# Where the expert-row buffer of a four-layer graph network is cleared: from the third layer's expert stage to the start of the program

## The chip, the cores and the metric

The kernel runs on one core of a Trainium2 chip. The metric is the device time of one execution in microseconds (us). Three runs of the kernel before gave 14256.97, 14292.15 and 14311.86 us, with a median of 14292.15 us.

## The reference, cut to what matters

Four layers follow each other over 3125 nodes with 256 float32 features and 100000 edges. Each layer is a graph part and a mixing part on the normalised nodes, and then an expert or token part. The change touches the third layer's expert part and the place where the edge lists are prepared.

```python
# third layer, expert part: E = 8 experts, hidden width 1024, the best two of 8 for each node
logits = xt @ Wr + br
probs = jax.nn.softmax(logits, axis=-1)
top_p, top_idx = jax.lax.top_k(probs, TOP_K)
weights = top_p / top_p.sum(axis=-1, keepdims=True)
...
xn = (xt - mu) * jax.lax.rsqrt(var + LN_EPS)
xe = xn[None, :, :] * ln_g[:, None, :] + ln_b[:, None, :]
h = jax.nn.gelu(jnp.einsum('end,edh->enh', xe, W1) + b1[:, None, :], approximate=False)
y = jnp.einsum('enh,ehd->end', h, W2) + b2[:, None, :]
sel = jnp.take_along_axis(y.transpose(1, 0, 2), top_idx[:, :, None], axis=1)
out = (weights[:, :, None] * sel).sum(axis=1)
```

The edges (`src`, `dst`, and two attributes `edge_attr_2` for each) are the same in all layers, so the kernel sorts them by target once, at the start.

## The kernel before, in words

`program` (L2413) holds the nodes in SBUF as X, 25 tiles of 125 nodes. It makes constants, loads x (`on_vector` "x_in", L886 with the load at L903), sorts the main edge list and the attention edge list (`sort_edges`, L107, tiles named em_ and eg_), lays out the sorted edges (`edge_rows`) and then runs eight stages in turn: the graph part and the expert part of each layer. The tiles of the stages have the prefixes a, b, c, d, e, f, g, h; the third layer's expert stage is f.

Each step of a stage is a `Block`: a piece of program for each engine, with semaphores between them. A block ends for all engines together: no engine begins the next block before every engine has got through its instructions of this one. That holds for the engine SP (SyncE) too, which does nothing but issue DMAs. It need not wait until a DMA has landed, but it must have issued it.

`sort_edges` begins with such a block. VectorE fills three tiles (L197 to L200); then SP issues the loads of `dst`, `src` and the attributes. Each array is spread over 128 partitions, 784 edges in each, which makes 127 full rows (L146, L150) and a shorter last row that is a DMA of its own (L148, L152). After these SP issues the fill of the list of edge slots in DRAM out of the tile em_pad (L154, 125 rows of 16000 bytes). VectorE waits for all six loads and then works out each edge's key (L206 on). All DMAs of SP go into one hardware queue, q1.

The third layer's expert stage, `layer2_experts` (L2193), sorts node rows by expert. Its buffers in DRAM are `f_sorted_in` and `f_sorted_out`, each 8192 + 256 = 8448 rows of 1024 bytes: 32 tiles of 256 rows, and 256 spare rows. A tile holds rows of one expert only, so some of its rows belong to no node and are cleared beforehand. The order of the stage is:

- the first block: VectorE clears the last 32 partitions of A (L2204); SP issues a DMA from one zero row in DRAM over all 8448 rows of `sorted_in` (L2208) and one over the last 256 rows of `sorted_out` (L2209), both counted on the semaphore `cleared`;
- `tile_norm` (`row_norm`, L1007 to L1018), `turn_rows` (L1047, L1056), `project` with the router's weights (loads L1088, matmuls L1098), softmax and the best two, `route` (L1936), which gives each node its two row numbers;
- the loads of the second weights w2 (L2232 to L2235), `tile_norm` on A, then `routed_rows` (L2021): GpSimd waits for `cleared` (L2033) and scatters the nodes' rows into `sorted_in` (L2036);
- `routed_experts` (L2040): 32 tiles of 256 rows through the two matrices; `joined_rows` (L2168) gathers the results.

`Scope` frees tiles and semaphores when a step ends; after 72 freed semaphores it clears them with one more barrier (L42).

Of the kernel before, what the change touches and what calls it, by code (L numbers as in the profile page):

```python
# [5 lines left out]
F32 = mybir.dt.float32  # L6
# [9 lines left out]
D = 256  # L16
# [1096 lines left out]
def put_rows(to, add=None):  # L1113

    def put(dve, t, bank, bias):
        at = to[0:NP, t, 0:bank.shape[-1]]
        if bias is not None:
            if add is None:
                return dve.tensor_tensor(at, bank, bias, ALU.add)
            dve.tensor_tensor(at, add[0:NP, t, :], bias, ALU.add)  # L1120
            dve.drain()
            return dve.tensor_tensor(at, bank, at, ALU.add)
        if add is not None:
            return dve.tensor_tensor(at, bank, add[0:NP, t, :], ALU.add)
        return dve.tensor_copy(at, bank)
    return put
# [387 lines left out]
def choose_two(nc, s, keep, lower, E, name):  # L1514
    with Scope(nc, name) as k:
        gt, eq, rank = k.sb("gt", [128, T, E, E]), k.sb("eq", [128, T, E, E]), k.sb("rank", [128, T, E])
        on_vector(nc, name, lambda dve: top_two(dve, s, gt, eq, rank, keep, lower, E))
# [75 lines left out]
def halves(xt):  # L1593
    return [xt[:, 0, :], xt[:, 1, :]]
# [338 lines left out]
F_ROOM = F_ROWS * F_TILES  # L1933
# [79 lines left out]
def expert_of(eng, tile_expert, i):  # L2013
    return eng.value_load(tile_expert[0:1, i:i + 1], min_val=0, max_val=7)


def load_first(sp, w1, w1_rows, e, i, loaded):
    sp.dma_start(w1[:, i % 2, :, :], w1_rows[bass.ds(e, 1), :, :].rearrange("a (q p) n -> p (a q) n", p=128)).then_inc(loaded[i % 2], 16)


def routed_rows(nc, A, slot, sorted_in, cleared, tile_expert, w1, w1_rows, loaded1):  # L2021

    with Scope(nc, "f_send") as k:
        scattered = k.own_sem("scattered")
        with nc.Block() as block:
            @block.sync
            def _(sp):
                for i in range(2):
                    load_first(sp, w1, w1_rows, expert_of(sp, tile_expert, i), i, loaded1)

            @block.gpsimd
            def _(pool):
                pool.wait_ge(cleared, 32)  # L2033
                for t in range(T):
                    for c in range(2):
                        pool.indirect_dma_start(sorted_in, bass.IndirectOffsetOnAxis(ap=slot[:, t, c:c + 1], axis=0), A[:, t, :], None).then_inc(scattered, 16)  # L2036
                pool.wait_ge(scattered, 16 * 2 * T)
# [152 lines left out]
                    dve.scalar_tensor_tensor(out=X[0:NP, t, :], in0=back[0:NP, n % RING, :], scalar=share[0:NP, t, c:c + 1], in1=X[0:NP, t, :], op0=ALU.mult, op1=ALU.add).then_inc(joined, 1)  # L2190


def layer2_experts(nc, I, X, const, lower):  # L2193
    with Scope(nc, "f") as k:
        gates, keep, A = k.sb("gates", [128, T, 8]), k.sb("keep", [128, T, 8]), k.sb("A", [128, T, D])
        w1, back = k.sb("w1", [128, 2, 2, 1024]), k.sb("back", [128, 8, D])
        sorted_in = nc.dram_tensor("f_sorted_in", (F_ROOM + 256, D), F32, kind="Internal").ap()
        sorted_out = nc.dram_tensor("f_sorted_out", (F_ROOM + 256, D), F32, kind="Internal").ap()
        cleared, loaded1, loaded2 = k.own_sem("cleared"), [k.own_sem(f"loaded1_{n}") for n in range(2)], k.own_sem("loaded2")
        slot, share, tile_expert = k.sb("slot", [128, T, 2], I32), k.sb("share", [128, T, 2]), k.sb("tile_expert", [1, F_TILES], I32)  # L2200
        with nc.Block() as block:
            @block.vector
            def _(dve):
                dve.memset(A[96:128, :, :], 0.0)  # L2204

            @block.sync
            def _(sp):
                sp.dma_start(sorted_in, I["zeros256"].to_broadcast([F_ROOM + 256, D])).then_inc(cleared, 16)  # L2208
                sp.dma_start(sorted_out[F_ROOM:F_ROOM + 256, :], I["zeros256"].to_broadcast([256, D])).then_inc(cleared, 16)  # L2209
        with Scope(nc, "f2") as j:  # L2210
            XT = j.sb("XT", [128, 2, N])
            tile_norm(nc, X, A, "f_norm")
            turn_rows(nc, A, XT, const, "f_turn")
            project(nc, halves(XT), I["L2_ffn_Wr"], 8, put_rows(gates), "f_g", bias=I["L2_ffn_br"])
            with Scope(nc, "f3") as s:
                total = s.sb("total", [128, T])
                softmax_of(nc, gates, 8, "f_s")
                choose_two(nc, gates, keep, lower[8], 8, "f_two")

                def shares(dve):  # L2220
                    dve.tensor_tensor(gates[0:NP, :, :], gates[0:NP, :, :], keep[0:NP, :, :], ALU.mult)
                    dve.drain()
                    normalise(dve, gates, total, 8)
                on_vector(nc, "f_sh", shares)
                route(nc, keep, gates, slot, share, tile_expert, const)
        with Scope(nc, "f4") as j:
            w2, b1, ln = j.sb("w2", [128, 8, 8, D]), j.sb("b1", [128, 8, 8]), j.sb("ln", [128, 2, 8, 2])
            with nc.Block() as block:
                @block.sync
                def _(sp):  # L2230
                    for e in range(8):
                        sp.dma_start(w2[:, e, :, :], I["L2_ffn_W2"][e, :, :].rearrange("(m p) n -> p m n", p=128)).then_inc(loaded2, 16)  # L2232
                    sp.dma_start(b1[:, :, :], I["L2_ffn_b1"].rearrange("e p m -> p e m")).then_inc(loaded2, 16)
                    sp.dma_start(ln[:, 0, :, :], I["L2_ffn_ln_g"].rearrange("e p m -> p e m")).then_inc(loaded2, 16)
                    sp.dma_start(ln[:, 1, :, :], I["L2_ffn_ln_b"].rearrange("e p m -> p e m")).then_inc(loaded2, 16)  # L2235
            tile_norm(nc, A, A, "f_norm2")
            routed_rows(nc, A, slot, sorted_in, cleared, tile_expert, w1, I["L2_ffn_W1"], loaded1)
            routed_experts(nc, sorted_in, sorted_out, w1, w2, b1, I["L2_ffn_W1"], I["L2_ffn_b2"], ln, tile_expert, A, loaded1, loaded2, const)
            joined_rows(nc, X, slot, share, sorted_out, back)
# [169 lines left out]
E_MAIN, J_MAIN, G_MAIN = 100000, 784, 125  # L2409
# [3 lines left out]
def program(nc, I, out):  # L2413
    with Scope(nc, "net") as k:
        const = dict(eye=k.sb("eye", [128, 128]), ones=k.sb("ones", [128, 128]), before=k.sb("before", [128, 128]),
                     ramp=k.sb("ramp", [128, 256]), up=k.sb("up", [128, 1]), zeros=k.sb("zeros", [1, 512]))
        lower = {4: k.sb("lower4", [128, 4, 4]), 8: k.sb("lower8", [128, 8, 8])}
        X, inv_deg = k.sb("X", [128, T, D]), k.sb("inv_deg", [128, T])
        main, gat = edge_list(nc, k, "main", G_MAIN, J_MAIN), edge_list(nc, k, "gat", G_GAT, J_GAT)
        constants(nc, const)  # L2420
        cut = k.sem("lower_cut")
        with nc.Block() as block:
            @block.gpsimd
            def _(pool):

                for n, E in enumerate((4, 8)):
                    pool.memset(lower[E][:, :, :], 1.0).then_inc(cut, 1)
                    pool.wait_ge(cut, n + 1)
                    pool.affine_select(out=lower[E][:, :, :], in_=lower[E][:, :, :], compare_op=ALU.is_gt, fill=0.0, base=0, pattern=[[1, E], [-1, E]], channel_multiplier=0)
        on_vector(nc, "x_in", lambda dve: None, loads=[(X[0:NP, :, :], table_rows(I["x"]))])  # L2430
        sort_edges(nc, main, I["src"], I["dst"], I["edge_attr_2"], E_MAIN, const, "em", inv_deg)
        sort_edges(nc, gat, I["gat_src"], I["gat_dst"], None, E_GAT, const, "eg")
        edge_rows(nc, k, main, const, "mr")
        stages = [lambda: layer0_graph(nc, I, X, inv_deg, main, const), lambda: layer0_experts(nc, I, X, gat, const, lower),
                  lambda: layer1_graph(nc, I, X, inv_deg, main, const), lambda: layer1_experts(nc, I, X, const, lower),
                  lambda: layer2_graph(nc, I, X, main, const), lambda: layer2_experts(nc, I, X, const, lower),
                  lambda: layer3_graph(nc, I, X, main, const), lambda: layer3_tokens(nc, I, X, const)]
        for stage in stages:
            stage()
        on_vector(nc, "x_out", lambda dve: None, stores=[(table_rows(out), X[0:NP, :, :])])  # L2440
# [53 lines left out]
```

## Time and profile before

| | |
|---|---|
| Runs of the kernel before | 14256.97, 14292.15, 14311.86 us |
| Execution that was profiled | 14272.68 us |
| Its span, first to last instruction | 14270.9 us |
| TensorE matmul busy | 7573.7 us (53%) |
| VectorE busy | 6386.1 us (45%) |
| GpSimd busy | 6037.2 us (42%) |
| ScalarE busy | 1225.8 us (9%) |
| Moved by DMA | 872.31 MB, 61 GB/s over the span |

All times of the trace are counted from the first instruction of the profiled execution. No engine is busy most of the time, because the stages follow each other and each is held by another engine. So a change is worth what it does to the length of the blocks it touches. A timeline row says when an instruction, or a run of equal ones, began, how long it took, and in brackets how long its engine had been idle and what ended the idle time; "<-PEq" and a line there is the end of a block. Rows marked SPq are SP issuing a DMA: their duration is the time that SP needed to issue it, not that of the transfer. In a table of windows the DMA share is the mean busy share of the 16 DMA engines.

### The profile page before, as it was taken

What the parts mean: (1) busy time and instruction counts of PE and PEld (TensorE: products, weight loads), DVE (VectorE), ACT (ScalarE), POOL (GpSimd) and SP (SyncE); (2) the same over time, 40 slices, a digit from 0 to 9 for tenths busy, and PEclk for the clock granted to TensorE, in tenths of its full rate; (3) what the DMA queues carried; (4) which work ended last, traced back from release to release, by engine and by line L of the source; (5) the groups of instructions that cost most, each with busy time, mean ns of one, the idle gap of its engine ahead of it and who ended that gap; (6) DMA issues with size and microseconds to landing.
All of it is one profiled execution on the core that took longest, in us unless ns stands there. A gap on an engine that the chain in (4) does not pass through costs nothing. (4 is left out here: it accounts for less than half of the span.)

```text
span 14270.9 us, 106989 instructions
## 1 busy us (share of the span) xinstructions
PE 7573.7 (53%) x30362; PEld 6003.4 (42%) x30362; DVE 6386.1 (45%) x16883; ACT 1225.8 (9%) x3131; POOL 6037.2 (42%) x6226
## 2 busy tenths in 40 slices
PE   3334432556665455685555564555571955666534
PEld 3333332345554355553343432433351844555423
DVE  6555654467885322320000434666632134444454
ACT  0000000000001100110000111000010210110001
POOL 1666465056662266306666003666501016666000
PEclk9999999767777555697777787777785977777767
DMA  1111111055664011103336001112503313336100
GB/s 40 55 50 56 36 55 40 19 166 170 173 176 84 10 8 8 11 23 93 92 92 85 10 6 31 45 45 46 39 9 81 111 62 95 94 94 89 26 8 15
DMA packets 455094, 872.31 MB, mean 61 GB/s; under 512 B 171930, under 2 KB 267396, under 8 KB 454154
## 3 DMA queue, kind: packets, MB, share of 16 engines
q0 software_dynamic: 277568, 621.62, 20.3%
q1 hardware_dynamic: 176960, 244.01, 5.6%
q8 instruction: 250, 4.10, 0.1%
q14 instruction: 316, 2.58, 0.1%
HBM read 821.23 MB, written 52.88 MB: 61 GB/s over the span
## 5 line engine op out<-in xcount | busy, mean ns | idle before, releaser
L552 POOL DMA_INDIRECT ee_rows<-e_table,net_mr_data x1000 | 993.5, 993 | 1271.9 <-POOLq L1405 691.3
L817 POOL DMA_INDIRECT ce_rows<-c_table,net_mr_data x1000 | 948.2, 948 | 979.8 <-SPq L810 505.8
L552 POOL DMA_INDIRECT ge_rows<-g_table,net_mr_data x1000 | 961.0, 961 | 670.8 <-issue 233.1
L387 POOL DMA_INDIRECT main_slots<-em_load,em_where x784 | 808.9, 1032 | 641.9 <-DVE em_where L362 388.5
L552 POOL DMA_INDIRECT ae_rows<-a_table,net_mr_data x752 | 726.2, 966 | 590.7 <-POOLq L1405 200.7
L552 POOL DMA_INDIRECT be_rows<-b_table,b_br_data x728 | 703.1, 966 | 428.7 <-issue 176.8
L589 PE MATMUL ee_part_ps<-ee_message,net_eye 125*125 125x256 f32 x2000 | 588.8, 459 | 451.2 <-issue 258.3
L589 PE MATMUL ge_part_ps<-ge_rows,net_eye 125*125 125x256 f32 x2000 | 626.8, 482 | 308.2 <-issue 163.3
L346 PE MATMUL em_look_ps<-em_table,em_hot_tT 25*128 25x125 f32 x1568 | 366.9, 421 | 732.1 <-issue 662.6
L828 PE MATMUL ce_part_ps<-ce_rows,net_eye 125*125 125x256 f32 x2000 | 599.2, 452 | 289.9 <-issue 195.7
L589 PEld LDWEIGHTS ee_part_ps<-ee_message,net_eye 125*125 125x125 f32 x2000 | 461.1, 235 | 560.2 <-issue 467.6
L387 POOL DMA_INDIRECT gat_slots<-eg_load,eg_where x512 | 530.3, 1036 | 387.6 <-DVE eg_where L362 226.8
L870 DVE TENSOR_TENSOR c_acc<-c_acc,ce_total_ps 125x512 f32 x125 | 86.0, 688 | 1342.2 <-remote 770.6
L589 PEld LDWEIGHTS ge_part_ps<-ge_rows,net_eye 125*125 125x125 f32 x2000 | 486.0, 250 | 418.3 <-issue 315.0
L346 PEld LDWEIGHTS em_look_ps<-em_table,em_hot_tT 25*128 25x128 f32 x1568 | 341.4, 325 | 756.9 <-issue 728.3
L828 PEld LDWEIGHTS ce_part_ps<-ce_rows,net_eye 125*125 125x125 f32 x2000 | 464.2, 233 | 400.4 <-issue 209.4
L346 PE MATMUL eg_look_ps<-eg_table,eg_hot_tT 25*128 25x125 f32 x1024 | 239.6, 421 | 472.5 <-issue 407.7
L589 PE MATMUL ae_part_ps<-ae_rows,net_eye 125*125 125x256 f32 x1504 | 423.0, 444 | 71.6 <-issue 41.8
L589 PE MATMUL be_part_ps<-be_rows,net_eye 125*125 125x16 f32 x1456 | 314.9, 365 | 262.7 <-issue 155.1
L614 PE MATMUL ae_total_ps<-ae_part,ae_hot 125*125 125x264 f32 x500 | 210.4, 561 | 441.8 <-issue 243.9
L724 DVE TENSOR_TENSOR ee_message<-ee_rows,ee_weight 125x512 f32<-125x512 f32 x500 | 309.6, 681 | 280.8 <-DMA em_key_row<-main_keys 276.6
L589 PEld LDWEIGHTS be_part_ps<-be_rows,net_eye 125*125 125x125 f32 x1456 | 314.4, 330 | 273.7 <-issue 272.1
(1010 smaller groups left out, 16655.6 us busy)
## 6 DMA issues: line engine op xcount, KB each, us to landing
em_key_row<-main_keys SPq DMA_DIRECT2D x98, 512.0 KB
f_w<-in_L_ffn_W_dram SPq DMA_DIRECT2D x40, 1024.0 KB
eg_key_row<-gat_keys SPq DMA_DIRECT2D x64, 512.0 KB
ce_rows<-c_table,net_mr_data POOLq DMA_INDIRECT x1000
ee_rows<-e_table,net_mr_data POOLq DMA_INDIRECT x1000
ge_rows<-g_table,net_mr_data POOLq DMA_INDIRECT x1000
main_slots<-em_load,em_where POOLq DMA_INDIRECT x784
ae_rows<-a_table,net_mr_data POOLq DMA_INDIRECT x752
```

The lines of the kernel that those rows point to most:

```text
L346: ins = pe.matmul(look_ps[i % 2][:, u, 0:NP], hot_tT[:, i % 2, u * 128:(u + 1) * 128], table[:, i % 2, u, 0:NP], start=True, stop=True)
L387: pool.indirect_dma_start(edge["slots"], bass.IndirectOffsetOnAxis(ap=where[:, c:c + 1], axis=0), load[:, c, :], None).then_inc(scattered, 16)
L552: pool.indirect_dma_start(rows[n][:, s, :], None, table, bass.IndirectOffsetOnAxis(ap=data[:, g, s, 0:1].bitcast(I32), axis=0)).then_inc(g ...
L589: pe.matmul(part_ps[0:NP, 0:VW], const["eye"][0:NP, 0:NP], values(g)[:, s, :], start=(s == 0), stop=(s == SLOTS - 1)).then_inc(slot_summed, 1)
L614: ins = pe.matmul(total_ps[0:NP, q, 0:WA], hot[0:NP, g % HOTS, q * NP:(q + 1) * NP], part[0:NP, g % PARTS, :], start=True, stop=True)
L724: ins = dve.tensor_tensor(message[0:NP, n, :, h * dv:(h + 1) * dv], r[0:NP, :, 0:dv], w[:, :, h:h + 1].to_broadcast([NP, SLOTS, dv]), ALU. ...
L817: pool.indirect_dma_start(rows[:, g % RING, s, :], None, table, bass.IndirectOffsetOnAxis(ap=data[:, g, s, 0:1].bitcast(I32), axis=0)).the ...
L828: pe.matmul(part_ps[g % 2][0:NP, 0:width], const["eye"][0:NP, 0:NP], rows[0:NP, g % RING, s, :], start=(s == 0), stop=(s == SLOTS - 1)).th ...
L870: dve.tensor_tensor(at, at, total_ps[g % 2][0:NP, :, 0:width], ALU.add).then_inc(added, 1)
```

## The change

The buffers and the semaphore `cleared` move from `layer2_experts` to `program`. After x has been loaded, a new block has VectorE fill a tile `blank` of 128 partitions x 22 x 256 float32 (22528 bytes in each partition) with zero. SP waits for that and issues four DMAs out of it: three over 2816 rows of `sorted_in` each, in which each partition writes 22 rows that lie behind each other, and one over the last 256 rows of `sorted_out`. Then `sort_edges` of the main list runs while `blank` still exists, and behind it a new block has SP wait for all four DMAs before the tile is given back. In the third layer's expert stage the two DMAs are gone; VectorE's clearing of A stays there. GpSimd's wait before the scatter is for 64 in place of 32.

```diff
@@ -2030,7 +2030,7 @@
-                pool.wait_ge(cleared, 32)
+                pool.wait_ge(cleared, 64)
@@ -2190,23 +2190,17 @@
-def layer2_experts(nc, I, X, const, lower):
+def layer2_experts(nc, I, X, const, lower, sorted_in, sorted_out, cleared):
...
-        sorted_in = nc.dram_tensor("f_sorted_in", (F_ROOM + 256, D), F32, kind="Internal").ap()
-        sorted_out = nc.dram_tensor("f_sorted_out", (F_ROOM + 256, D), F32, kind="Internal").ap()
...
             @block.vector
             def _(dve):
                 dve.memset(A[96:128, :, :], 0.0)
 
-            @block.sync
-            def _(sp):
-                sp.dma_start(sorted_in, I["zeros256"].to_broadcast([F_ROOM + 256, D])).then_inc(cleared, 16)
-                sp.dma_start(sorted_out[F_ROOM:F_ROOM + 256, :], I["zeros256"].to_broadcast([256, D])).then_inc(cleared, 16)
@@ -2428,12 +2422,33 @@
         on_vector(nc, "x_in", lambda dve: None, loads=[(X[0:NP, :, :], table_rows(I["x"]))])
-        sort_edges(nc, main, I["src"], I["dst"], I["edge_attr_2"], E_MAIN, const, "em", inv_deg)
+        sorted_in = nc.dram_tensor("f_sorted_in", (F_ROOM + 256, D), F32, kind="Internal").ap()
+        sorted_out = nc.dram_tensor("f_sorted_out", (F_ROOM + 256, D), F32, kind="Internal").ap()
+        cleared = k.own_sem("cleared")
+        with Scope(nc, "blank") as j:
+            share = (F_ROOM + 256) // 128 // 3
+            blank, made = j.sb("blank", [128, share, D]), j.sem("made")
+            with nc.Block() as block:
+                @block.vector
+                def _(dve):
+                    dve.memset(blank[:, :, :], 0.0).then_inc(made, 1)
+
+                @block.sync
+                def _(sp):
+                    sp.wait_ge(made, 1)
+                    for n in range(3):
+                        sp.dma_start(sorted_in[n * share * 128:(n + 1) * share * 128, :].rearrange("(p a) w -> p a w", p=128), blank[:, :, :]).then_inc(cleared, 16)
+                    sp.dma_start(sorted_out[F_ROOM:F_ROOM + 256, :].rearrange("(p a) w -> p a w", p=128), blank[:, 0:2, :]).then_inc(cleared, 16)
+            sort_edges(nc, main, I["src"], I["dst"], I["edge_attr_2"], E_MAIN, const, "em", inv_deg)
+            with nc.Block() as block:
+                @block.sync
+                def _(sp):
+                    sp.wait_ge(cleared, 64)
         sort_edges(nc, gat, I["gat_src"], I["gat_dst"], None, E_GAT, const, "eg")
```

## Rows read from the trace of the kernel before

**Rows 1.** Windows by stage: us, busy of each engine, clock, DMA share, GB/s
```profile
core 0: us, PE busy (x) PEld busy (x) DVE busy (x) ACT busy (x) POOL busy (x), PEclk, DMA share, GB/s
...
10716.00:10819.00 103.00, 0.00 (x0) 0.00 (x0) 5.42 (x2) 0.07 (x1) 0.00 (x0) 0.50 0.47 67
10819.00:11021.00 202.00, 30.46 (x154) 29.61 (x154) 65.09 (x279) 20.30 (x37) 48.32 (x51) 0.52 0.37 95
11021.00:11530.00 509.00, 466.22 (x2176) 400.86 (x2176) 59.06 (x128) 122.65 (x257) 0.04 (x1) 0.99 0.31 104
```

**Rows 2.** Timeline at the border from stage e to stage f
```profile
10708.26 6.83 DVE L1473 TENSOR_TENSOR net_X<-net_X,e_B 125x6400 f32<-125x6400 f32 x1 [0.32 <-PEq L1179]
10715.45 0.59 SPq L2208 DMA_DIRECT2D f_sorted_in<-in_zeros_dram  x1
10716.09 102.19 SPq L2209 DMA_DIRECT2D f_sorted_out<-in_zeros_dram  x1
10716.85 5.39 DVE L2204 MEMSET f_A<- 32x6400 f32 x1 [1.77 <-issue]
10818.93 1.28 ACT L999 ACT_TABLE_LOAD   x1 [124.52 <-PEq L2201]
10818.97 8.27 DVE L1007 BATCH_NORM_STATS2 f_norm_stats<-net_X 125x6 f32<-125x256 f32 x25 [96.72 <-PEq L2201]
```

**Rows 3.** Instructions on f_sorted_in: the clear and its time to landing
```profile
L2208 SPq DMA_DIRECT2D f_sorted_in<-in_zeros_dram x1: 592/592/592, 10715.5 to 10715.5; - x1
...
DMA to landing us min/median/max: 130.0/130.0/130.0
```

**Rows 4.** Timeline later in stage f: the router's loads and matmuls, GpSimd's first scatter
```profile
10845.17 0.38 SPq L1088 DMA_DIRECT2D f_g_w<-in_L_ffn_Wr_dram  x1
10845.60 0.36 SPq L1088 DMA_DIRECT2D f_g_b<-in_L_ffn_br_dram  x1
10848.63 21.17 PE L1098 MATMUL f_g_bank<-f_g_w,f_XT 128*125 128x8 f32 x100 [4.22 <-DMA f_g_b<-in_L_ffn_br_dram]
...
10951.69 1.00 POOL L2036 DMA_INDIRECT f_sorted_in<-f_A,f_slot  x1 [61.04 <-PEq L2025]
```

**Rows 5.** Timeline at the border from stage c to stage d
```profile
8329.15 6.83 DVE L1029 TENSOR_TENSOR net_X<-net_X,c_B 125x6400 f32<-125x6400 f32 x1
8337.42 8.27 DVE L1007 BATCH_NORM_STATS2 d_norm_stats<-net_X 125x6 f32<-125x256 f32 x25 [1.45 <-PEq L42]
```

**Rows 6.** Timeline at the start: the end of x's load, the edge loads, the first keys
```profile
36.45 0.71 DVE L197 MEMSET em_dst_i<- 128x784 int32 x1 [33.05 <-PEq L899]
...
39.68 0.24 SPq L146 DMA_DIRECT2D em_dst_i<-in_dst_dram  x1
...
40.43 2.67 DVE L202 MEMSET em_load<- 128x3136 f32 x1 [0.80 <-issue]
...
103.56 0.57 DVE L206 CAST em_key<-em_dst_i 128x784 f32<-128x784 int32 x1 [59.35 <-DMA em_at<-in_edge_attr_dram]
...
118.15 1.76 PE L179 MATMUL em_turn_ps<-net_eye,em_key 128*128 128x128 f32 x7 [118.15 <-DVE em_work L223]
```

**Rows 7.** Windows of single transfers: DMA share and GB/s are the last two columns
```profile
41.40:83.40 42.00, 0.00 (x0) 0.00 (x0) 2.69 (x3) 0.00 (x0) 2.76 (x2) 1.00 0.06 26
86.00:100.00 14.00, 0.00 (x0) 0.00 (x0) 0.00 (x0) 0.00 (x0) 0.00 (x0) 1.00 0.31 129
10720.00:10845.00 125.00, 7.62 (x50) 7.37 (x50) 21.33 (x74) 11.20 (x21) 0.00 (x0) 0.52 0.54 68
10908.00:10924.00 16.00, 0.00 (x0) 0.00 (x0) 0.00 (x0) 0.00 (x0) 0.00 (x0) 0.50 1.07 345
2820.00:2860.00 40.00, 0.00 (x0) 0.00 (x0) 0.00 (x0) 0.00 (x0) 0.00 (x0) 0.50 0.33 127
```

**Rows 8.** Windows of the sort of the main list and of the pause behind it
```profile
277.00:1500.00 1223.00, 463.25 (x2356) 415.43 (x2356) 641.43 (x3627) 98.20 (x98) 808.94 (x784) 1.00 0.18 52
1475.00:1521.00 46.00, 0.00 (x0) 0.00 (x0) 14.16 (x23) 0.00 (x0) 21.05 (x20) 1.00 0.11 38
```

More of the change, by code:

```diff
@@ L2196, in layer2_experts @@
         w1, back = k.sb("w1", [128, 2, 2, 1024]), k.sb("back", [128, 8, D])
-        sorted_in = nc.dram_tensor("f_sorted_in", (F_ROOM + 256, D), F32, kind="Internal").ap()
-        sorted_out = nc.dram_tensor("f_sorted_out", (F_ROOM + 256, D), F32, kind="Internal").ap()
-        cleared, loaded1, loaded2 = k.own_sem("cleared"), [k.own_sem(f"loaded1_{n}") for n in range(2)], k.own_sem("loaded2")
+        loaded1, loaded2 = [k.own_sem(f"loaded1_{n}") for n in range(2)], k.own_sem("loaded2")
         slot, share, tile_expert = k.sb("slot", [128, T, 2], I32), k.sb("share", [128, T, 2]), k.sb("tile_expert", [1, F_TILES], I32)
@@ L2435, in program @@
                   lambda: layer1_graph(nc, I, X, inv_deg, main, const), lambda: layer1_experts(nc, I, X, const, lower),
-                  lambda: layer2_graph(nc, I, X, main, const), lambda: layer2_experts(nc, I, X, const, lower),
+                  lambda: layer2_graph(nc, I, X, main, const), lambda: layer2_experts(nc, I, X, const, lower, sorted_in, sorted_out, cleared),
                   lambda: layer3_graph(nc, I, X, main, const), lambda: layer3_tokens(nc, I, X, const)]
```

## The prediction

> **What bounds the kernel now.** The chain that ended last covers only the closing 200 us, so I read the program stage by stage. First I took the windows by stage [rows 1]. The reader is to see a hole: from 10716 to 10819 us TensorE, ScalarE and GpSimd do next to nothing and VectorE is busy for 5.42 us. Then the timeline of that border [rows 2]. SP issues the clear of sorted_in in 0.59 us, and the second, small DMA then takes 102.19 us to issue: it has to get in behind the first one's descriptors. A block ends only when SP has got through it, so VectorE, done with its MEMSET at 10716.85 + 5.39 = 10722.24, sits idle for 96.72 us and starts the next norm at 10818.97. The clear bounds this block, though nobody needs the cleared rows yet. GpSimd's scatter begins at 10951.69, released by the end of the block before it (PEq L2025) [rows 4], 106 us after the clear has landed: 10715.5 + 130.0 = 10845.5 [rows 3].
>
> At the other place, the start, the timeline [rows 6] shows VectorE waiting 59.35 us for the edge loads, until 103.56, with every other engine idle. So that block is bound by DMA, and what matters is which DMA engine. From 41.4 to 83.4 us the share is 0.06 at 26 GB/s [rows 7]: that is one engine of 16. From 86 to 100 us the loads overlap with the em_pad store at a share of 0.31, five engines of 16, and 129 GB/s, again 26 for each. The loads have 127 rows and em_pad has 125, and 127 is prime, so one and five engines are what an even split gives. The six loads hold 400000 + 400000 + 800000 = 1.6 MB, which at 26 GB/s is 61.5 us. Counted back from 103.56, less some 0.6 us for the landing, they start to flow at 41.4, about 1.7 us behind the first issue at 39.68. This one engine, E0 below, sets the end of the block.
>
> **What the change removes.** In stage f's first block the MEMSET of A stays and ends at 10722.24. Between two blocks VectorE needs 0.32 us (the first line of [rows 2]) when nothing else is late. Where semaphores are cleared as well it needs 1.45 us [rows 5]. So the norm can start at 10722.6, and 10818.97 - 10722.6 = **96.4 us** go, with 95.2 as the other bound. What is late next is nothing: that norm reads X, ready since 10715.09, and ScalarE's table load of 1.28 us lies beside VectorE's 8.27 us of statistics. The router's loads were issued at 10845.17 and 10845.60 and TensorE started at 10848.63 [rows 4]; they sat behind the clear's last descriptors by at most a microsecond (3.0 us from the second issue to the first matmul), which I cost at nothing. Behind that the stage shifts as a whole. GpSimd's wait for 64 is met 10 ms before it is asked, so its cost is nothing.
>
> **What the change adds at the start.** Four terms.
> (1) VectorE's MEMSET of 5632 elements in each partition. The one of 3136 took 2.67 us [rows 6], 0.85 ns for an element, so 4.8 us. No other work lies beside it, since x has just landed and the next block has not begun. It runs from 36.45 to 41.25.
> (2) Four issues by SP. Issues into a free queue took 0.24 us and 0.59 us [rows 2, 6]; 4 x 0.4 = 1.6 us. I cost no backlog, since a DMA of 128 rows over 16 engines gives each only 8 rows; the second clear before had 528 rows of the first in each engine ahead of it. With 0.35 us for the end of the block the sort's first instruction moves from 36.45 to about 43.3, so 6.9 us later. The first edge load is then issued at about 46.6.
> (3) The transfer. The clears flow from 41.3 + 1.7 = 43.0. The bytes are (8448 + 256) x 1024 = 8.91 MB, and 128 rows divide evenly over 16 engines, so E0 carries 0.557 MB of them. The edge loads are queued behind on the same queue. I take it that E0 works in the order of issue, so the loads begin to flow when E0's part of the clears is done, in place of 41.4. What does E0's part cost? No row shows 16 engines writing to DRAM at once. With few engines each writes 26 GB/s (em_pad; five engines at 127 GB/s for a_table with rows of 2 KB [rows 7]): 21.4 us. With all 16 busy, reading weights, the rate was 345 GB/s, 21.6 each [rows 7]: 25.8 us. I take 23.5, between the two nearest rows. The loads then start at 43.0 + 23.5 = 66.5, and their end moves by 66.5 - 41.4 = **25.1 us**. This contains terms (1) and (2), it is not added to them: the 3.6 us from the clears' flow to the first load's issue lie beside the transfer. The bounds are 23.0 and 27.4.
> (4) The closing block after the sort: the clears have landed over 1 ms before, so only a block's end remains, 0.4 us, or 1.5 us if the one more freed semaphore moves a semaphore clear.
> The em_pad store waits behind the loads on E0 as before and ends before the keys' stores; this moves along with the rest. What stands behind the wait for the loads is VectorE's chain from L206 to L223, and TensorE behind it at 118.15 [rows 6]: all of it moves by the same time.
>
> The Trainium skill bears on (3) twice. Its page "DMA: Bandwidth & Descriptors", in the section "Queues, rings and completion order", says that on each DMA engine descriptors are consumed in ring order; no row here shows two different transfers of one queue overtaking or not, so by that rule term (3) stands as it is and rival A falls. The same page's section "Bandwidth" gives some 358 GB/s as what HBM grants one core: 8.91 MB / 358 GB/s is an estimate of 24.9 us for the clears and would make the sum -69.5 in place of -70.9. The 345 GB/s of the row lies close to it, for reads.
>
> **The sum.** -96.4 + 25.1 + 0.4 = **-70.9 us**, with bounds of about -73.0 (-96.4 + 23.0 + 0.4) and -66.3 (-95.2 + 27.4 + 1.5). Made against the profiled execution this is 14272.68 - 70.9 = 14201.8 us. The profiled execution lies 19.5 us below the median of the runs; from the median the sum gives 14221.3. The four executions of before spread over 55 us and neither is the better base, so I take the middle, 14212 us.
>
> **The rivals.**
> A: the edge loads don't wait. If E0 shared its time between the clears and the loads or took the loads first, only the 6.9 us of (1) and (2) and the 0.4 of (4) would be paid: -96.4 + 7.3 = -89.1 us, 14183.6 to 14203.1 by the two bases. For it speaks that E0's loads are small rows beside large ones; against it that both are on one queue, and that the router's loads, issued when the clear was just landing, came no sooner than it [rows 3, 4]. Chance 0.10.
> B: sixteen engines can't write to DRAM that fast. Then the clears take longer on every engine: at 127 GB/s, the most that any store here reached, 70 us, which ends E0's part at 113 and moves the loads by 71.8: -96.4 + 71.8 + 0.4 = -24.2 us. At 200 GB/s, between that and 345, they take 44.6 us, and it gives -49.8. For it speaks that no row shows a faster store; against it that those stores used five engines of 16 and ran at the full rate of each. Chance 0.17. Times of 14223 to 14268.
> C, the other side: the buffer's rows take writes at no more than the clear's own rate before, 68 GB/s at a DMA share of 0.54 [rows 7]. Before it was unseen whether that was the one zero row being read 8448 times or the writes. If the writes, the clears take 131 us again and now lie wholly in front of the edge loads: 43.0 + 131 - 41.4 = 132.6, so -96.4 + 132.6 + 0.4 = +36.6 us, 14309 to 14329. It decides for slower below 8.91 MB / 94.4 us = 94 GB/s. Against it stand 127 to 129 GB/s of stores with only five engines. Chance 0.03.
> D: the sort loses its clock. TensorE is granted 1.00 (2.4 GHz) through the whole sort, after 118 us of idling and again through 46 us of it [rows 8]; now the first idling lasts 143 us. If it fell to 0.50 (1.2 GHz), TensorE's 463 us of work in the main list's sort would double, part of it behind VectorE: +200 us or more. Nothing in the rows points there. Chance 0.03.
> E: the change does not do what it says, because stage f's first block is held by something the profile does not name, or a barrier elsewhere grows by tens of us. Chance 0.03; I would see about no change.
>
> **How the numbers follow.** My forecast has 0.62. A measurement of this kernel can tell about 0.5% from no change, here 71.4 us. The forecast of -70.9 lies right at that line, so I split it evenly: 0.31 faster by over 0.5%, 0.31 within. A goes to faster (0.10), B to within (0.17), C with +36.6 us to within (0.03), D to slower (0.03), E to within (0.02) and to slower (0.01). The last 0.02 go to faster, for a gain that I don't see. Faster 0.43, within 0.53, slower 0.04. The range: downwards it takes in A from the lower base, 14183.6, as half of its chance; upwards it takes in B down to about 200 GB/s from the median, 14242, and some way on. From 14182 to 14255 I leave out some 0.18: the slow half of B, C, D, E and a part of A.
>
> **What would show it.** Right: VectorE's idle time before f_norm_stats falls from 96.72 us to 0.3 to 1.5. The first SP issue of stage f is the router's load. At the start a MEMSET of 4.8 us and four short issues stand at 36 to 43 us, a window at a DMA share near 1 with 350 to 410 GB/s follows, then 0.06 and 26 GB/s again until about 128, and L206 starts at about 128.7. The sort keeps its 1.00 clock. Wrong: L206 near 111 speaks for A; a window of clears at 130 to 200 GB/s and L206 past 150 for B; one at 68 for C. A second clear-issue that takes tens of microseconds would mean that my term (2) is wrong and that the stall has moved with the clear.

## The result and the profile after

The changed kernel took 14197.08 us (median of 6 runs, 14175.68 to 14208.54) against 14289.05 us before (6 runs, 14247.58 to 14311.86). The ratio is 0.9932 with a 95% interval from 0.9912 to 0.9951: 97 us less, between 70 and 126. (Here and below, a gain in us is the ratio applied to the median of before; the two medians themselves are 92 us apart.) The profiled executions are 14272.68 and 14191.58 us, 81.1 us apart. The forecast was 14212 us and -70.9 us.

The border from stage e to stage f, in the timeline of the kernel after, answers to [rows 2]:

```profile
10718.53 6.83 DVE L1473 TENSOR_TENSOR net_X<-net_X,e_B 125x6400 f32<-125x6400 f32 x1 [0.32 <-PEq L1179]
10727.13 5.39 DVE L2202 MEMSET f_A<- 32x6400 f32 x1 [1.77 <-issue]
10732.79 1.28 ACT L999 ACT_TABLE_LOAD   x1 [28.10 <-PEq L2199]
10732.82 8.27 DVE L1007 BATCH_NORM_STATS2 f_norm_stats<-net_X 125x6 f32<-125x256 f32 x25 [0.30 <-PEq L2199]
```

SP issues nothing here any more and VectorE's idle time before the norm is 0.30 us in place of 96.72. From the end of the addition to X until the norm's first instruction it was 10818.97 - 10715.09 = 103.88 us and is 10732.82 - 10725.36 = 7.46: 96.4 us less.

The start, which answers to [rows 6]:

```profile
37.40 4.75 DVE L2434 MEMSET blank_blank<- 128x5632 f32 x1 [34.00 <-issue]
42.18 1.78 SPq L2440 DMA_DIRECT2D f_sorted_in<-blank_blank  x3
44.00 1.26 SPq L2441 DMA_DIRECT2D f_sorted_out<-blank_blank  x1
...
45.90 0.71 DVE L197 MEMSET em_dst_i<- 128x784 int32 x1 [3.75 <-PEq L2431]
...
49.13 0.27 SPq L146 DMA_DIRECT2D em_dst_i<-in_dst_dram  x1
49.46 19.66 SPq L148 DMA_DIRECT2D em_dst_i<-in_dst_dram  x1
...
127.01 0.57 DVE L206 CAST em_key<-em_dst_i 128x784 f32<-128x784 int32 x1 [73.36 <-DMA em_at<-in_edge_attr_dram]
```

The first edge load is issued 9.5 us later than before, and the second then takes 19.66 us to issue in place of 6.17, with the clears ahead of it. The first key is worked out at 127.01 in place of 103.56, 23.45 us later. Windows of the kernel after, which answer to [rows 7] (the last two columns are the DMA share and GB/s):

```profile
44.00:60.00 16.00, 0.00 (x0) 0.00 (x0) 6.45 (x6) 1.28 (x1) 7.82 (x4) 1.00 1.00 428
70.00:104.00 34.00, 0.00 (x0) 0.00 (x0) 0.00 (x0) 0.00 (x0) 0.00 (x0) 1.00 0.06 26
110.00:120.00 10.00, 0.00 (x0) 0.00 (x0) 0.00 (x0) 0.00 (x0) 0.00 (x0) 1.00 0.31 131
```

All 16 DMA engines write at 428 GB/s, 26.8 each. Then one engine alone carries the edge loads at 26 GB/s again, and em_pad goes over five.

Where the difference between the two profiled executions lies (81.1 us in device time, 81.2 us in their spans), by the first instruction of each stage (us):

| Stretch | before | after | difference |
|---|---|---|---|
| start to the count of the main sort (L249) | 129.0 | 152.5 | +23.5 |
| main sort and closing block | 1399.8 | 1407.7 | +7.9 |
| second sort, rows of edges | 954.1 | 948.0 | -6.1 |
| stages a to d | 6179.7 | 6192.2 | +12.5 |
| stage e, with the first block of stage f | 2156.4 | 2032.4 | -124.0 |
| the rest of f, g, h, the output | 3451.9 | 3456.9 | +5.0 |

The edit explains +23.5, of the +7.9 some 0.4 (GpSimd's idle time before the second sort grew from 10.29 to 10.69 us), and 96.4 of the 124.0. The other 27.6 us in stage e have no counterpart in the edit.

### The profile page after: what moved, and what is told of

Same layout as the page of the kernel before. It is cut to its first block and busy times, and to the rows that moved or that the text cites. A ratio compares the mean times of both kernels' runs of the same rounds, so it can differ in the third digit from the quotient of the medians.

```text
span 14189.7 us, 107005 instructions
## 1 busy us (share of the span) xinstructions
PE 7583.6 (53%) x30362; PEld 6009.5 (42%) x30362; DVE 6397.2 (45%) x16884; ACT 1227.0 (9%) x3131; POOL 6040.0 (43%) x6226
## 5 line engine op out<-in xcount | busy, mean ns | idle before, releaser
L589 PE MATMUL ae_part_ps<-ae_rows,net_eye 125*125 125x256 f32 x1504 | 421.7, 443 | 74.8 <-ACT ae_part L650 40.0
L346 PEld LDWEIGHTS eg_look_ps<-eg_table,eg_hot_tT 25*128 25x128 f32 x1024 | 222.9, 325 | 484.2 <-issue 443.4
```

Of the source, the lines that this page charges most:

```text
L346: ins = pe.matmul(look_ps[i % 2][:, u, 0:NP], hot_tT[:, i % 2, u * 128:(u + 1) * 128], table[:, i % 2, u, 0:NP], start=True, stop=True)
L589: pe.matmul(part_ps[0:NP, 0:VW], const["eye"][0:NP, 0:NP], values(g)[:, s, :], start=(s == 0), stop=(s == SLOTS - 1)).then_inc(slot_summed, 1)
```

## The experiments

Two questions were open. Do the two terms carry the whole gain, or is there a further 20 us? And is each of the two what I took it for: the old clear slow by its source, the new cost the work of one DMA engine in the order of issue? The time of the kernel before differs from chip to chip (13099 and 13103 us on two, 14253 to 14289 on the others), so each run is compared with the kernel before on its own chip.

**The changed kernel again (after_again).** No edit.

> The changed kernel once more, against the kernel before, to see whether the trace's two terms carry the whole gain. Theory T1 (nothing but the two terms that the traces show): 96.4 us less in stage f's first block, 23.5 us more until the first key is worked out and about 0.4 for the closing block, so 72 to 73 us faster in all, ratio 0.995, and everything else differs from one execution to the next with no sign. Theory T2 (a further gain of some 20 us that the edit brings somewhere else): about 92 us faster, ratio 0.9935 or below, and the same stage is the shorter one in both profiles of the changed kernel. In the profile both expect the first key at 127.0 (+-0.5) and VectorE idle for 0.3 us before the third expert stage's norm.

13036.96 us against 13102.69, ratio 0.9948 (0.9934 to 0.9961): -68 us, between -51 and -86. The first key came at 127.16 us. This is T1; the -92 us of T2 lie outside the interval.

**Both clears (e2_both_clears).** The addition alone.

```diff
+            @block.sync
+            def _(sp):
+                sp.dma_start(sorted_in, I["zeros256"].to_broadcast([F_ROOM + 256, D])).then_inc(cleared_late, 16)
+                sp.dma_start(sorted_out[F_ROOM:F_ROOM + 256, :], I["zeros256"].to_broadcast([256, D])).then_inc(cleared_late, 16)
...
-                pool.wait_ge(cleared, 64)
+                pool.wait_ge(cleared_late, 32)
```

> The addition alone: the new clears at the start stay, and stage f clears its buffers as well, as the kernel before did. T1: +23.5 until the first key and 0.4 for the closing block, 24 us slower than before in all (ratio 1.0017), with the 96.7 us of idle VectorE back in stage f. T2, if the further gain hangs on the early clear: about no change (+4 us); if it hangs on the removal: +24 as T1.

13131.53 us against 13102.69, ratio 1.0023 (1.0013 to 1.0032): +30 us, between +17 and +42. VectorE's wait in stage f was back at 98.7 us and the first key came at 126.97:

```profile
DVE f_norm_stats L1007 <- PEq L2199: 98.7, 1, 98.7
```

The addition costs what the trace's 23.5 + 0.4 says. The early clear brings no gain elsewhere.

**Clears behind the stores (e5_behind_stores).** The removal with next to no addition.

```diff
                     pool.memset(pad[:, :, 1], -1e6).then_inc(padded, 1)
+                    pool.memset(blank_rows[:, :, :], 0.0).then_inc(padded, 1)
...
+                    sp.wait_ge(padded, 2)
+                    for to_rows, of_rows in clears:
+                        sp.dma_start(to_rows, of_rows).then_inc(zeroed, 16)
                     sp.wait_ge(filled, 16)
                     sp.wait_ge(kept, 32 * BLOCKS)
```

> The same clears out of SBUF, but issued by SP behind the stores of keys and tiles, where the trace shows no DMA until 277 us; GpSimd, idle then, fills the zero tile. So the removal is left with nearly no addition. T1: the first key back at 103.6 us, the block of the first keys longer by SP's four issues, 2 to 3 us, the closing block 0.4: -96.4 + 3 = -93 us (ratio 0.9935). T2 with the further gain on the removal: -113 us. A rival to my term for the transfer: if the clears delay the first loads of the main sort's second phase or the edge loads after all, less than 80 us are gained.

13006.91 us against 13102.69, ratio 0.9930 (0.9917 to 0.9944): -92 us, between -73 and -109. The first key is back at its old place, and the count begins 2.2 us later than in the kernel before:

```profile
44.02 4.86 POOL L177 MEMSET blank_blank<- 128x5632 f32 x1
...
103.50 0.57 DVE L212 CAST em_key<-em_dst_i 128x784 f32<-128x784 int32 x1 [59.28 <-DMA em_at<-in_edge_attr_dram]
...
127.40 1.85 SPq L163 DMA_DIRECT2D f_sorted_in<-blank_blank  x3
129.29 1.26 SPq L163 DMA_DIRECT2D f_sorted_out<-blank_blank  x1
...
131.15 0.17 DVE L255 MEMSET em_ones<- 25x128 f32 x1 [10.70 <-PEq L141]
```

So the 24 us that the change pays at the start are a matter of whether the clears are issued before the edge loads or behind them.

**Short rows (e11_short_rows).** The changed kernel with 1 KB pieces, out of the same tile.

```diff
-...rearrange("(p a) w -> p a w", p=128), blank[:, :, :])
+...rearrange("(a p) w -> p a w", p=128), blank[:, :, :])
```

> The changed kernel, in which each partition writes single rows of 1 KB that lie 128 rows apart, in place of one run of 22 KB: 8704 pieces in place of 26 to each engine. It parts two causes of the 68 GB/s of the old clear. If it was the one zero row in DRAM that all pieces read (my view): the pieces flow at 350 to 420 GB/s, the clears take 21 to 26 us, the first key is at 127 to 132 us; SP is held in the block for some of that. If it was the short rows in DRAM: about 68 GB/s, 131 us, and the first key near 236 us.

The expectation has a slip: 8704 pieces are the total. By the program each engine gets 544 of them, in place of 32 (8 partitions in each of four DMAs). The window (DMA share and GB/s last):

```profile
44.00:60.00 16.00, 0.00 (x0) 0.00 (x0) 0.00 (x0) 0.00 (x0) 0.00 (x0) 1.00 1.04 344
```

This is one execution, read by its trace. The rate is 344 GB/s, and the first key comes at 132.34, 5.3 us later than with long runs. SP was held for 13.16 and 8.27 us by its issues. Short rows cost a fifth of the rate (428 to 344), not the factor of six down to 68. So rows of 1 KB in DRAM were not what held the old clear.

**The zero row at the start (e3_zero_row_early).**

```diff
-                    dve.memset(blank[:, :, :], 0.0).then_inc(made, 1)
...
+                    sp.dma_start(sorted_in, I["zeros256"].to_broadcast([F_ROOM + 256, D])).then_inc(cleared, 32)
+                    sp.dma_start(sorted_out[F_ROOM:F_ROOM + 256, :], I["zeros256"].to_broadcast([256, D])).then_inc(cleared, 32)
```

> The clears at the start, but by the two old DMAs from the zero row in DRAM; no zero tile is filled. It prices the part of the change that the move alone would not have brought. T1 (the one zero row in DRAM is the limit, wherever the clear stands): 68 GB/s, 131 us; SP is held for 102 us in the new block, the edge loads flow only when the clears are done, at about 169, and the first key is worked out at 169 + 61.5 + 0.6 = 231 us, 127 us later than before; in all -96.4 + 127 + 0.4 = +31 us against before. Rival (the clear was slow only in stage f, by something beside it there): the rate is above 200 GB/s here, the first key before 145 us.

One execution, 14313.3 us against a median of 14252.84 before (7 runs, 14245.2 to 14284.55): +60 us. The first key came at 230.39 us:

```profile
36.12 0.63 SPq L2434 DMA_DIRECT2D f_sorted_in<-in_zeros_dram  x1
36.80 102.96 SPq L2435 DMA_DIRECT2D f_sorted_out<-in_zeros_dram  x1
...
230.39 0.57 DVE L206 CAST em_key<-em_dst_i 128x784 f32<-128x784 int32 x1 [81.89 <-DMA em_at<-in_edge_attr_dram]
```

```profile
60.00:100.00 40.00, 0.00 (x0) 0.00 (x0) 0.00 (x0) 0.00 (x0) 0.00 (x0) 1.00 0.31 68
```

68 GB/s as in stage f [rows 7], and the stall of 102 us moved with it. The DMA share is 0.31 here and was 0.54 there at the same rate; no run asked why. Moving the old clear without changing its source would have made the kernel slower: by the trace -96.4 + 126.8 + 0.4 = +31 us, as expected. The +60 us of this single execution are more, and the other 29 are not explained. With e11 this leaves the source: one zero row in DRAM that 8448 pieces read. Whether that is the single address, or a transfer from DRAM to DRAM as such, these two runs do not part.

**SBUF source at the old place (e4_sbuf_late).** The kernel before, with the source alone changed.

```diff
+                dve.memset(blank[:, :, :], 0.0).then_inc(made, 1)
                 dve.memset(A[96:128, :, :], 0.0)
...
-                sp.dma_start(sorted_in, I["zeros256"].to_broadcast([F_ROOM + 256, D])).then_inc(cleared, 16)
+                for n in range(3):
+                    sp.dma_start(sorted_in[n * 22 * 128:(n + 1) * 22 * 128, :].rearrange("(p a) w -> p a w", p=128), blank[:, :, :]).then_inc(cleared, 16)
```

> The clears stay in stage f, but come out of a zeroed SBUF tile with runs of 22 KB instead of from the zero row in DRAM. It asks whether the move to the start was needed at all. T1: the second DMA's 102 us of issue are gone, SP is through in 3 us beside VectorE's fill of A, and the transfer of 21 us lies beside the norm (18 us) and ends before the router's loads are issued. Only the fill of 4.75 us is added: -96.4 + 4.8 = -92 us (ratio 0.993), 20 us better than the change. Rival: the clears delay something of stage f, for instance the router's loads, by their 21 us: -75 us.

14171.08 us against 14261.51, ratio 0.9937 (0.9912 to 0.9962): -90 us, between -54 and -126. The timeline of its first block:

```profile
10707.47 6.83 DVE L1473 TENSOR_TENSOR net_X<-net_X,e_B 125x6400 f32<-125x6400 f32 x1 [0.32 <-PEq L1179]
10715.92 4.75 DVE L2205 MEMSET f_blank<- 128x5632 f32 x1 [1.62 <-issue]
10720.70 1.78 SPq L2212 DMA_DIRECT2D f_sorted_in<-f_blank  x3
10722.06 5.39 DVE L2206 MEMSET f_A<- 32x6400 f32 x1 [1.39 <-issue]
10722.52 1.25 SPq L2213 DMA_DIRECT2D f_sorted_out<-f_blank  x1
10727.72 1.28 ACT L999 ACT_TABLE_LOAD   x1 [34.09 <-PEq L2202]
10727.75 8.27 DVE L1007 BATCH_NORM_STATS2 f_norm_stats<-net_X 125x6 f32<-125x256 f32 x25 [0.30 <-PEq L2202]
```

From the end of the addition to X to the norm 13.45 us pass in place of 103.88, 90.4 less. The gain of the change is the gain of its source; the place at the start costs 18 us against this one by the traces (-72.5 against -90.4). The timed intervals of the two overlap, so that difference rests on the timelines. The rival of the expectation does not show: from this norm to stage g's, 782.7 us pass, against 779.8 before and 781.8 after.

**Clears directly behind the edge loads (e8_behind_loads).** As e5, but SP issues them behind the store of em_pad and ahead of the stores of keys and tiles.

> The clears out of SBUF issued by SP directly behind the edge loads and the em_pad store, ahead of the stores of keys and tiles; GpSimd fills the zero tile. It asks whether a DMA engine works in the order of issue, by what then waits. T1 (order of issue on each engine): the first key is back at 103.5 us; the lowest engine has em_pad until 119 and then 21 us of clears, so its parts of the keys' and tiles' stores, issued from 121 us on, land near 142 and the count begins at 143 to 144 in place of 129.0: 14 to 15 us later, so -96.4 + 15 = -81 us in all (ratio 0.9938 to 0.9945). Rival A (an engine takes later transfers of the queue alongside): the count begins at 131 to 133, and -92 us as with the clears behind the stores.

14192.29 us against 14261.51, ratio 0.9958 (0.9941 to 0.9976): -60 us, between -34 and -84. The first key is back at its old place, and then:

```profile
84.56 10.89 SPq L158 DMA_DIRECT2D f_sorted_in<-blank_blank  x3
95.50 2.14 SPq L158 DMA_DIRECT2D f_sorted_out<-blank_blank  x1
103.29 0.57 DVE L212 CAST em_key<-em_dst_i 128x784 f32<-128x784 int32 x1 [59.27 <-DMA em_at<-in_edge_attr_dram]
...
120.65 18.97 SPq L163 DMA_DIRECT2D main_keys<-em_turned  x7
...
139.66 7.74 SPq L163 DMA_DIRECT2D main_tiles<-em_turned  x7
...
149.74 0.17 DVE L255 MEMSET em_ones<- 25x128 f32 x1 [29.49 <-PEq L141]
```

The stores of keys, issued in 3.19 us elsewhere, took SP 18.97 us, and the count begins 20.7 us later than in the kernel before, where rival A had 2 to 4. So transfers issued behind the clears wait for them. But SP was held while it issued them, so this run alone doesn't part an engine that works in order from a queue that takes no more. My 15 us were too few, since I let the stores be issued and only land late; SP's own stall came on top.

The order on one queue shows better in the landing of the last clear (`sorted_out`). In e4, with nothing issued behind it until it has landed, that took 21.2 us. In the changed kernel the first edge load is issued 5 us behind it, and it took 21.3:

```profile
L2441 SPq DMA_DIRECT2D f_sorted_out<-blank_blank x1: 1264/1264/1264, 44.0 to 44.0; - x1
...
DMA to landing us min/median/max: 21.3/21.3/21.3
```

The load took next to nothing from the clears.

**Split edge loads (e6_split_loads, e9_split_before, e7_split_behind_stores).** The 127 rows of each edge load in two DMAs, in the changed kernel, in the kernel before, and together with the clears behind the stores.

```diff
+            pieces = [(0, full)] if full % 16 == 0 else [(0, full // 16 * 16), (full // 16 * 16, full)]
...
-                        sp.dma_start(to[0:full, :], of[0:full * J].rearrange("(p j) -> p j", j=J)).then_inc(loaded, 16)
+                        for p0, p1 in pieces:
+                            sp.dma_start(to[p0:p1, :], of[p0 * J:p1 * J].rearrange("(p j) -> p j", j=J)).then_inc(loaded, 16)
```

> The changed kernel with each edge load of 127 rows cut into one of 112 rows and one of 15. It asks whether the 61.5 us behind the clears are the work of a single DMA engine because 127 is prime. T1: 112 rows go over 16 engines and 15 over 15, the loads take 4 to 5 us behind the clears in place of 61.5, the first key is worked out at about 70 us in place of 127, and the whole is -72 - 57 = -129 us against before (ratio 0.990). Rival: the rate of 26 GB/s comes from something else than one engine (short rows, the source): the first key stays at 120 us or later and the whole near -72.

> The kernel before with nothing changed but the edge loads cut into 112 and 15 rows each; the clear stays in stage f from the zero row. With the two other runs it says whether the terms add up. T1: the loads take 4 to 5 us in place of 61.5, the first key at 49 us and the count at 75 us as in the version with both edits, -54 us (ratio 0.9962). Rival (some of the other versions' gain was not where I put it): less than 40 us, or more than 70.

> Both: the edge loads cut into 112 and 15 rows, and the clears behind the stores of keys and tiles. The version that should be fastest. T1: loads from 41.4 to about 46, first key at about 47 us (56 us earlier than before), the count at about 75 instead of 129, the rest as with the clears behind the stores: -93 - 56 = -149 us (ratio 0.9886). If em_pad's 16 us on five engines end later than the keys need, or GpSimd's fills (until 49 us) hold the store of em_pad, up to 10 us less.

| | first key | count begins | us | ratio to before | in us |
|---|---|---|---|---|---|
| after, loads split (e6) | 71.6 | 97.1 | 14128.07 | 0.9911 (0.9879 to 0.9942) | -127 (-83 to -173) |
| before, loads split (e9) | 49.3 | 74.8 | 14181.9 | 0.9943 (0.9926 to 0.9960) | -81 (-57 to -105) |
| loads split, clears behind the stores (e7) | 49.2 | 76.8 | 14108.55 | 0.9902 (0.9877 to 0.9927) | -140 (-104 to -175) |

The timeline of e7, the fastest kernel of the study:

```profile
44.31 0.26 SPq L157 DMA_DIRECT2D main_slots<-em_pad  x1
49.18 0.57 DVE L215 CAST em_key<-em_dst_i 128x784 f32<-128x784 int32 x1 [4.86 <-DMA em_at<-in_edge_attr_dram]
```

VectorE's wait for the edge loads is 4.86 us in place of 59.35. The loads that took one engine 61.5 us take some 7 on sixteen (an estimate: from 1.7 us behind their first issue at 39.81 to 0.6 us ahead of the key), where 4 to 5 were expected. Together with the DMA share of 0.06 this shows that 127 rows went through one engine.

e6 and e7 lie near their expectations (-129 and -149 us). e9 does not: its -81 us fall into the band of the rival (more than 70), and the interval, which ends at -57, leaves out the 54 us by which the count begins earlier. Its profiled execution is 81 us below that of the kernel before too, and 17 of these lie in the stage e of the table above (2139.2 in place of 2156.4 us), whose code it does not touch. So the 54 us of its timeline are shown; the other 27 are not explained.

**Clears on ScalarE's queue (e10_act_queue, e10_again).**

```diff
-                @block.sync
+                @block.scalar
                 def _(sp):
                     sp.wait_ge(made, 1)
```

> The changed kernel with the clears issued by ScalarE, on its own hardware queue, and the edge loads by SP as before. It asks whether the delay of the loads is a matter of one queue's order or of the one engine's work. T1 (work of one engine: 0.557 MB of clears and 1.6 MB of loads pass it in whatever order): the first key at 126 to 128 us, as with one queue; the loads begin earlier and run slower beside the clears. Rival A in another form (loads of another queue go first or alongside without loss): first key at 104 to 115 us.

The first key came at 126.81 us. The last clear now landed 23.8 us after its issue in place of 21.3, so here the loads did take something from the clears, and yet the delay of the first key is the same 23 us:

```profile
L2441 ACTq DMA_DIRECT2D f_sorted_out<-blank_blank x1: 1274/1274/1274, 44.0 to 44.0; - x1
...
DMA to landing us min/median/max: 23.8/23.8/23.8
...
126.81 0.57 DVE L206 CAST em_key<-em_dst_i 128x784 f32<-128x784 int32 x1 [73.18 <-DMA em_at<-in_edge_attr_dram]
```

The one engine has both to carry: 0.557 + 1.6 = 2.16 MB at 26 GB/s are 83 us, and from 43.9 that ends at 127, in whatever order. That is T1. This execution as a whole took 14790.44 us, 537 more than before, with TensorE at a granted clock of 0.75 in the third expert stage where [rows 1] shows 0.99:

```profile
11300.00:11400.00 100.00, 99.02 (x355) 71.44 (x354) 9.22 (x20) 20.69 (x44) 0.00 (x0) 0.75 0.24 83
```

So the same kernel was timed again.

> The same kernel as the one with the clears on ScalarE's queue, timed. Its one look took 537 us more than before, all of it behind the sort: TensorE was granted 0.75 in the third expert stage in place of 0.99 and a matmul took 482 ns in place of 379. T1 (that execution or chip had a lower clock, the edit has no part in it): here the granted clock of that stage is back near 0.99 and the ratio at 0.995, as for the changed kernel. Rival (using ScalarE's DMA queue once costs clock or TensorE rate for the rest of the program): about +500 us again, ratio 1.035.

The median is 13035.17 us against 13098.94. Four of the five executions lie between 13025 and 13043 us and give the ratio of 0.9947 (0.9930 to 0.9963): -69 us, as the changed kernel. So ScalarE's queue does not always cost 500 us. The fifth, which was the one profiled, took 15786.54 us. In it the granted clock of the third expert stage was 0.56, not near 0.99, and its matmuls (L2107) took 566 ns in the median:

```profile
12200.00:12300.00 100.00, 99.88 (x268) 58.93 (x267) 7.38 (x16) 14.67 (x31) 0.00 (x0) 0.56 0.21 69
```

Two of six executions of this kernel were long in this way, and none of over 100 of the other kernels in this study. Whether the queue has a part in that stays open.

## Why the prediction was right

**The removal** was 96.4 us, as worked out from the two rows and the gap of 0.3 us between blocks. e4 shows it too: 90.4 with 4.75 us of fill added. What was late next was nothing, as said.

**Terms (1) and (2).** The fill took 4.75 us against 4.8. The sort's first instruction came 9.45 us later, not 6.9: VectorE began the fill 0.95 us late, the four issues took 3.1 us in place of 1.6 (1.26 of it the fourth), and the block's end 0.6. The late fill moves the start of the clears too and so is part of term (3). The rest cost nothing, because the transfer covers it, as the sum had it. So did the 19.66 us for which SP was held at the second load, a backlog that the prediction did not have: the first load was already queued.

**Term (3)** was 23.45 us, inside the bounds of 23.0 and 27.4 and below the 25.1 that I took. The transfer was mis-sized by being placed between two rows: 20.8 us in place of 23.5, with a start 0.9 us later. It ran at 428 GB/s, 26.8 for each engine, which is the row of the few engines that write and not that of the sixteen that read. In 1 KB pieces the same clears ran at 344 (e11), so for these stores the length of the pieces and not the number of busy engines set the lower rate. The weights of [rows 7], read in rows of 1 KB, ran at 345, so most likely the same holds for them; no run changed that load. The Trainium skill's some 358 GB/s of HBM for a core ("DMA: Bandwidth & Descriptors", "Bandwidth"), which that section ties to both cores of a pair streaming, was not the limit here: this kernel on one core wrote 428. The order of issue that the same page states ("Queues, rings and completion order") agrees with the last clear's landing in 21.3 us with a load behind it, against 21.2 with none.

**Term (4)** was 0.4 us.

**The sum** of the edit's own terms is -96.4 + 23.5 + 0.4 = -72.5 us; forecast -70.9. The first comparison measured 97 us less, the second 68. The stretch from stage e's norm to stage f's norm, taken without the 96.4 us of the clear where it stands there and without the 4.8 of e4, was 2060.0, 2032.4, 2071.5, 2060.8, 2024.4, 2025.6, 2072.0 and 2042.8 us in the kernels before, after, e8, e4, e6, e7, e3 and e9, whose code for stage e is the same. After and the two versions that have both the new clears and split loads are low, e8 and e3, which clear early too, are high. On the chip of after_again it scatters less: 1793.5 us there, 1783.6 in e5 and 1793.4 in e11. So the 27.6 us of stage e in the first pair are most likely such scatter; what causes it was not tried. The measured 14197 us thus lie 15 us below the forecast for a reason that the sum does not have. That they are still inside the range is partly luck: it reached down to 14182 only for the sake of rival A, which did not come. The chance split evenly at the line of 0.5% was fair: the first ratio lies beyond it, the second (-0.52%) on it.

**The rivals.** A fell by the first key at 127.01 in place of 111, and its price was wrong in one of its two forms. Only if E0 takes the loads first is -89 us right. If it shares its time, the loads, which are the larger part of its work, still end when all 2.16 MB are through, at about 127; e10 shows that case. B and C fell with the 428 GB/s of the new clears; C's question is answered, since e3 had 68 GB/s at the start too and e11 344 with the same short rows from SBUF. D did not come (1.00 through the sort), and its price was wrong as well, see below. E fell with VectorE's 0.30 us.

What the prediction missed was not in its numbers but in its scope. It priced the move and the new source as one. e3 and e4 show that the source brings the gain and that the move costs some of it.

## What to carry to other kernels

When one small DMA takes 100 us to issue, look at what stands ahead of it in its queue, and at the source of that: a clear out of a zeroed SBUF tile ran six times as fast as one that repeats a row of DRAM. Before moving a transfer to a quiet place, find the DMA engine that sets the end of the block there, from the share of the 16 engines together with the rate (0.06 at 26 GB/s was one engine, 0.31 at 129 GB/s five; the old clear in e3 stood at 0.31 as well, but at 68 GB/s, so the share alone does not tell): new work costs what it puts on that engine, whatever queue it comes from. A row count with no large divisor up to 16 kept transfers on few engines here (127 rows on one, 125 on five, 128 on all); cutting 127 rows into 112 and 15 was worth over 50 us here, twice the cost that the change had paid.

## What the runs showed of the hardware that was not expected

A granted clock of 0.50 in the profile need not mean slower matmuls. In the sort of e5 the clock stands at 0.50 from 300 to 1300 us, as in that of e11 (main sort 1240.2 us), in that of after_again on the same chip at 1.00. The matmuls of the lookup took the same in both, 412 ns in the median, and the main sort 1239.4 and 1239.3 us:

```profile
300.00:1300.00 1000.00, 450.30 (x2295) 403.92 (x2293) 607.60 (x3541) 95.10 (x95) 751.30 (x752) 0.50 0.20 60
```

```profile
300.00:1300.00 1000.00, 465.79 (x2356) 415.41 (x2356) 624.14 (x3629) 98.33 (x99) 738.82 (x739) 1.00 0.21 64
```

In the third expert stage of e10 the clock of 0.75 did go with longer matmuls, 482 ns in the median against 379 in the kernel before. So rival D priced an event that in e5 and e11 took place and cost nothing. The reverse stands in the profiled execution of e10_again: its lookup took 534 ns in the median with the clock at 1.00. So the matmul times, not the clock alone, say how fast TensorE ran.

The kernel before took about 13100 us on two chips and 14253 to 14289 on the others. After_again and after, the same kernel, took 13037 and 14192 us in their profiles: the main sort 1239.3 and 1407.7 us, and the second sort, stages a, b, c, e and g were longer too, while stages d, f and h were not (325.8 and 325.8, 782.3 and 781.8, 410.7 and 410.0 us). Why, no run here asked.
